# Combine and the last layer's attention in one pipeline, the context's LayerNorm beside the expert tiles

## The reference

```python
# layer 0, tail: combine the two experts' outputs of each token
eo = einsum('etf,efd->etd', gelu(einsum('td,edf->etf', x2, w1) + b1), w2) + b2
x3 = layernorm(x2 + sum_over_top2(weight[t, e] * eo[e, t]), ln3_g, ln3_b)
# layer 1, head: both sides of the attention are normalised with the same gain and shift
q_in = layernorm(x3, ln1_g, ln1_b)
kv_in = layernorm(ctx, ln1_g, ln1_b)
x4 = x3 + attention(q_in, kv_in, kv_in)      # 16 heads of 8, softmax over 64 keys
out = x4 + mlp(layernorm(x4, ln2_g, ln2_b))
```

## Time and profile before

| | |
|---|---|
| median of 3 runs | 1650.91 us (1648.1 to 1655.75) |
| the profiled execution, its own time | 1651.23 us |
| its span, first to last instruction | 1649.5 us |
| busy share of the span | PE 79%, PEld 65%, DVE 63%, ACT 56%, POOL 54% |
| mean granted TensorE clock | 0.882 of full |
| HBM traffic | 95.45 MB read, 50.86 MB written, 89 GB/s |

### The profile page before, as it was taken

How to read it: one execution, slowest core, us unless ns; L and a number is a source line. 1 busy time by engine, 2 the same in 40 slices (tenths; PEclk the granted TensorE clock), 3 DMA queues, 4 the chain that set the end, 5 groups by cost and what they waited for, 6 DMA issues and landing times. The chain is left out here.

```text
span 1649.5 us, 60559 instructions
## 1 busy us (share of the span) xinstructions
PE 1295.0 (79%) x23128; PEld 1068.0 (65%) x23128; DVE 1045.7 (63%) x2321; ACT 918.7 (56%) x1624; POOL 896.5 (54%) x1424
## 2 busy tenths in 40 slices
PE   5999999999999465799999980111138999994998
PEld 3787877778877364699999970111116788873676
DVE  4777777778878229677777762656636788782011
ACT  2787877788887305533333331544446788872333
POOL 2576767576676300477777737567504666753111
PEclk9999999999999757899999995555558999997899
DMA  3233333333332160022222213555522233321333
GB/s 104 83 91 102 89 101 93 104 91 103 107 95 72 46 211 0 22 65 61 61 60 60 60 45 97 136 144 144 150 96 65 86 107 102 96 78 43 106 114 90
DMA packets 169853, 147.65 MB, mean 90 GB/s; under 512 B 19105, under 2 KB 132257, under 8 KB 169761
## 3 DMA queue, kind: packets, MB, share of 16 engines
q1 hardware_dynamic: 161312, 129.11, 26.0%
q0 software_dynamic: 8448, 17.32, 4.5%
HBM read 95.45 MB, written 50.86 MB: 89 GB/s over the span
## 5 line engine op out<-in xcount | busy, mean ns | idle before, releaser
L741 DVE TENSOR_REDUCE at_mx<-at_ps_s 128x16 f32<-128x1024 f32 x128 | 156.1, 1220 | 104.5 <-PE at_ps_s L490 60.1
L1339 POOL DMA_INDIRECT ex_xg<-x,ex_ti x136 | 164.8, 1211 | 46.3 <-issue 44.6
L678 ACT ACTIVATE at_pt<-at_ps_t 128x1024 f32<-128x1024 f32 x128 | 130.6, 1020 | 52.5 <-PE at_ps_t L504 51.7
L1368 PE MATMUL ex_ps_y<-ex_wt,ex_hg 128*128 128x128 f32 x1088 | 157.2, 288 | 2.8 <-ACT ex_hg L1399 2.8
L671 ACT ACTIVATE at_pr<-at_dd 128x1024 f32<-128x1024 f32 x128 | 135.2, 1056 | 35.3 <-DVE at_dd L749 35.3
L749 DVE TENSOR_TENSOR at_dd<-at_ps_s,at_mx 128x1024 f32<-128x1024 f32 x128 | 153.7, 1202 | 0.1
L1551 POOL DMA_INDIRECT cb_yg<-rows,cb_sl x128 | 125.8, 983 | 44.4 <-issue 44.0
L1368 PEld LDWEIGHTS ex_ps_y<-ex_wt,ex_hg 128*128 128x128 f32 x1088 | 131.6, 191 | 26.0 <-ACT ex_hg L1399 21.8
L1359 PE MATMUL ex_ps_h<-ex_xt,ex_wt 128*128 128x128 f32 x1088 | 146.2, 278 | 0.0
L1391 ACT ACTIVATE ex_xt<-ex_ps_x 128x128 f32<-128x128 f32 x136 | 37.7, 277 | 193.8 <-issue 99.1
L504 PE MATMUL at_ps_t<-ident,at_pr 128*128 128x128 f32 x1024 | 138.9, 279 | 4.8 <-issue 3.3
(11 more groups left out here) (237 smaller groups left out, 3419.0 us busy)
## 6 DMA issues: line engine op xcount, KB each, us to landing
rows<-ex_y SPq DMA_DIRECT2D x136, 64.0 KB
x<-at_ln_out SPq DMA_DIRECT2D x32, 256.0 KB, 3.2
at_kx<-in_xt SPq DMA_DIRECT2D x16, 256.0 KB, 2.8
at_qx<-in_xt SPq DMA_DIRECT2D x16, 256.0 KB, 2.8
at_vin<-in_xt SPq DMA_DIRECT2D x16, 256.0 KB, 2.8
at_xr<-in_x SPq DMA_DIRECT2D x16, 256.0 KB, 3.0
x1t<-at_xt SPq DMA_DIRECT2D x16, 256.0 KB, 3.3
at_kx<-in_ctxt SPq DMA_DIRECT2D x16, 256.0 KB, 2.8
```

The source lines that it names most:

```text
L678: act.activation(pt[:, 2 * h + p], ps_t[:, :, :, :], ACT.Copy).then_inc(pt_ready, 1)
L741: dve.tensor_reduce(mx[:, p], ps_s[:, :, 4 * p:4 * p + 4, :], AX.X, ALU.max).then_inc(mx_ready, 1)
L1339: pool.indirect_dma_start(out=xg[:, s, :], out_offset=None, in_=x_src, in_offset=bass.IndirectOffsetOnAxis(ap=ti[:, s:s + 1], axis=0)).the ...
L1368: mm = pe.matmul(ps_y[s % 2][:, :], hg[:, s % 2, f, :], wt[:, s % HB, W2 + D * f:W2 + D * f + D], start=(f == 0), stop=(f == FC - 1))
```

## The change

combine_phase is gone. Its context part moves into expert_phase, once in each of the first 16 rounds of 8 tiles; the rest moves into a new fused_phase together with the last attention.

In the expert phase, round q normalises group q of the context: SP loads it at the round's first tile, VectorE takes statistics and moments at tiles 1 and 2, GpSimd computes the reciprocal root behind the gather of tile 7, ScalarE scales in two halves at tiles 4 and 5, TensorE transposes at tile 6, ScalarE copies at tile 7, SP stores. The PSUM bank for it comes from ps_h, which has 2 buffers in place of 4.

In the fused phase there are steps from -4 to 18. In step g the front of the pipeline weighs group g+4, finishes x3 of g+3 and z4 of g+2, whose transpose stays on the chip (qx) in place of going through HBM; the attention works on g, g-1 and g-2, and the last transpose is that of g-3. GpSimd fetches group g+5 in four portions between its other work, computes own and next LayerNorm's root together (front_rstd, eight columns), and no longer masks: ScalarE applies the head masks as scale and bias while it copies K and Q out of PSUM, in two passes each (kb, qb doubled). The context's group is loaded once for K and V. x3 goes to HBM and comes back for the residual. vx, ot, LayerNorm's out are doubled. The Sqrt and the Newton step are gone.

The diff, cut, in this order: the steps' loop; then, of fused_phase, the step of TensorE, two helpers and the step of ScalarE, a helper and the step of VectorE, two helpers and the step of GpSimd; then, of expert_phase, GpSimd, TensorE, ScalarE and VectorE; then the phases' calls. `prior`, `here`, `following` and `more` say whether group g-1, g, g+1 and g+2 exist, `front` whether g+4 does.

```diff
+def over_steps(eng, step, end):
...
+    for g in range(-4, 4):
+        step(At(1, g))
+    with eng.Fori(2, end // 2) as m:
+        for u in range(2):
+            step(At(1, m * 2 + u, 0, m * 2 + u, u, m))
+    for g in range(end, NG + 3):
+        step(At(1, g))
...
+                    if prior:
+                        turn(g * 2 - 1, 1, 1)
+                    if following:
+                        project_q(a.shift(1))
+                    if here:
+                        scores(a, 1)
+                        turn(g * 2, 0, 0)
+                    if prior:
+                        widen(g * 2 - 2, 0)
+                    if more:
+                        if following:
+                            pe.wait_ge(qb_ready, g + 2)
+                        else:
+                            pe.wait_ge(bob_ready, 1)
+                        project_k(a.shift(2))
+                    if prior:
+                        values(a.shift(-1), 1)
+                    if here:
+                        turn(g * 2, 0, 1)
+                    if following:
+                        if more:
+                            pe.wait_ge(kb_ready, g + 3)
+                        else:
+                            pe.wait_ge(qb_ready, g + 2)
+                        project_v(a.shift(1))
+                        scores(a.shift(1), 0)
+                    if a.shift(-3).exists():
+                        if following:
+                            pe.wait_ge(vx_ready, g + 2)
+                        elif a.shift(-2).exists():
+                            pe.wait_ge(y_ready, g - 1)
+                        else:
+                            pe.wait_ge(xt_ready, NG - 1)
+                        turn_x(a.shift(-3))
+                    if prior:
+                        widen(g * 2 - 1, 1)
+                    if here:
+                        turn(g * 2 + 1, 1, 0)
+                    if prior:
+                        if beyond(g, 2):
+                            pe.wait_ge(xt_ready, g - 2)
+                        else:
+                            pe.wait_ge(vx_ready, g + 2)
+                        project_out(a.shift(-1))
+                    if here:
+                        values(a, 0)
+                    if more:
+                        if prior:
+                            pe.wait_ge(y_ready, g)
+                        elif following:
+                            pe.wait_ge(vx_ready, g + 2)
+                        else:
+                            pe.wait_ge(kb_ready, g + 3)
+                        turn_z(a.shift(2))
...
+                def mask_q(a):
...
+                    for f in range(2):
+                        ins = act.activation(qb[:, a.u, :, f, :], ps_g[:, :].rearrange("p (b q) -> p b q", b=GB),
+                                             ACT.Identity, bias=side[:, 0, f:f + 1], scale=c.side[:, f:f + 1])
+                    ins.then_inc(qb_ready, 1)
...
+                def scale_next(a):
+
+                    act.wait_ge(fnb_ready, a.g + 2)
+                    if beyond(a.g, 1):
+                        act.wait_ge(z4t_ready, a.g - 1)
+                    front_scale(z4[:, a.u], x3[:, a.u], a.shift(1), NEXT).then_inc(fz_ready, 1)
...
+                    if following:
+                        copy_z(a.shift(1))
+                    if prior:
+                        exponent(g * 2 - 1, 1)
+                        copy_t(g * 2 - 1, 1, 0)
+                    if here:
+                        exponent(g * 2, 0)
+                    if prior:
+                        copy_t(g * 2 - 1, 1, 1)
+                    if following:
+                        mask_q(a.shift(1))
+                    if prior:
+                        copy_o(g * 2 - 2, 0)
+                    if here:
+                        exponent(g * 2, 1)
+                        copy_t(g * 2, 0, 0)
+                    if a.shift(3).exists():
+                        scale_own(a.shift(3))
+                    if a.shift(2).exists():
+                        mask_k(a.shift(2))
+                    if here:
+                        exponent(g * 2 + 1, 0)
+                        copy_t(g * 2, 0, 1)
+                    if following:
+                        copy_v(a.shift(1))
+                    if a.shift(-3).exists():
+                        copy_x(a.shift(-3))
+                    if prior:
+                        copy_o(g * 2 - 1, 1)
+                    if a.shift(2).exists():
+                        scale_next(a.shift(2))
+                    if a.shift(-2).exists():
+                        ln.act_scale(act, a.shift(-2))
+                over_steps(act, step, NG - 4)
...
+                def weigh_first(a):
+
+                    dve.wait_ge(yg_in[a.u], 16 * 2 * GP * (a.k + 1))
+                    dve.wait_ge(in_f[a.u], 32 * (a.k + 1))
+                    for t in range(GP):
+                        ins = dve.scalar_tensor_tensor(y1[:, a.u, t, :], yg[:, a.u, 0, t, :], wt[:, a.u, 0, t:t + 1],
+                                                       fx[:, a.u, t, :], ALU.mult, ALU.add)
+                    ins.then_inc(y1_ready, 1)
+
...
+                    if here:
+                        subtract(g * 2, 1)
+                    if a.shift(-2).exists():
+                        ln.dve_statistics(dve, a.shift(-2), y_ready)
+                    if prior:
+                        recip(g * 2 - 2, 0)
+                    if a.shift(-2).exists():
+                        ln.dve_moments(dve, a.shift(-2))
+                    if here:
+                        maximum(g * 2 + 1, 0)
+                    if prior:
+                        normalise(a.shift(-1), 0)
+                    if here:
+                        subtract(g * 2 + 1, 0)
+                    if front:
+                        weigh_first(a.shift(4))
+                    if here:
+                        maximum(g * 2 + 1, 1)
+                    if prior:
+                        recip(g * 2 - 1, 1)
+                    if here:
+                        subtract(g * 2 + 1, 1)
+                    if front:
+                        weigh_second(a.shift(4))
+                    if a.shift(3).exists():
+                        gain_own(a.shift(3))
+                    if following:
+                        maximum(g * 2 + 2, 0)
+                    if prior:
+                        normalise(a.shift(-1), 1)
+                    if a.shift(3).exists():
+                        shift_own(a.shift(3))
+                    if following:
+                        maximum(g * 2 + 2, 1)
+                        subtract(g * 2 + 2, 0)
+                    if front or a.shift(3).exists():
+                        front_statistics(a.shift(4))
+                    if prior:
+                        residual(a.shift(-1))
+                    if front or a.shift(3).exists():
+                        front_moments(a.shift(4))
...
+                def fetch_close(a):
+
+                    pool.wait_ge(fy_ready, a.g + 1)
+                    tick(2 + a.u)
...
+                def front_rstd(a):
+                    pool.wait_ge(fmv_ready, a.g + 1)
+                    if beyond(a.g, 1):
+                        pool.wait_ge(z3_ready, a.g - 1)
+                    if beyond(a.g, 2):
+                        pool.wait_ge(fz_ready, a.g - 2)
+                    pool.tensor_tensor(fneg[:, a.u, :], fmv[:, a.u, :, 0], c.minus_one[:, 0:2 * GP], ALU.mult)
+                    pool.tensor_tensor(frstd[:, a.u, :], fmv[:, a.u, :, 1], c.eps[:, 0:2 * GP],
+                                       ALU.add).then_inc(fvar_ready, 1)
+                    pool.wait_ge(fvar_ready, a.g + 1)
+                    pool.tensor_tensor(frstd[:, a.u, :], frstd[:, a.u, :], c.minus_half[:, 0:2 * GP],
+                                       ALU.pow).then_inc(frstd_ready, 1)
+                    pool.wait_ge(frstd_ready, a.g + 1)
+                    pool.tensor_tensor(fnb[:, a.u, :], fneg[:, a.u, :], frstd[:, a.u, :], ALU.mult).then_inc(
+                        fnb_ready, 1)
...
+                    nearby = a.shift(5)
+                    if a.shift(3).exists() or a.shift(2).exists():
+                        front_rstd(a.shift(3))
+                    if nearby.exists():
+                        fetch_open(nearby)
+                        fetch(nearby, 0, 1)
+                    if prior:
+                        spread(g * 2 - 2, 0)
+                    if nearby.exists():
+                        fetch(nearby, 1, 3)
+                    if a.shift(-2).exists():
+                        ln.pool_rstd(pool, a.shift(-2))
+                    if nearby.exists():
+                        fetch(nearby, 3, 5)
+                    if prior:
+                        spread(g * 2 - 1, 1)
+                    if nearby.exists():
+                        fetch(nearby, 5, 8)
+                    if a.shift(-2).exists():
+                        gain(a.shift(-2))
+                    if here:
+                        add_bias(a)
...
```

(33 more changed lines are left out.)

798 lines of the change are left out of this document (516 added, 282 removed).

## The result

| | median us | runs | ratio to before |
|---|---|---|---|
| before | 1651.97 (1648.1 to 1655.75) | 4 | |
| after | 1703.39 (1697.37 to 1705.57) | 4 | 1.0306 [1.0268, 1.0344] |
| predicted | 1567 (1528 to 1612) | | |

The change makes the kernel 3.1% slower; 5% faster was forecast. The profiled execution of after took 1705.57 us for a span of 1703.8.

What follows compares the result with a forecast made beforehand. GpSimd was taken to bound the fused stage. Experts ending at 1022.1 us, the fused stage at 1423.5 and the remaining 141.8 gave a span of 1565.3; with 1.7 outside it, 1567 us, range 1528 to 1612.

Steps and rivals of the forecast that it cites:

- The costly piece is an order on GpSimd's queue: Experts: the root waits for VectorE's moments, delaying the next gather; stall 1.4 us in a round of 2.3, 37 us total.
- part 1: The context's normalisation beside the expert tiles: 2.3 us a round, 16 rounds, 37 us.
- The upper bound of 55 us: Experts: the most part 1 could cost, if a whole weight copy held up both gather and root.
- The ring: Fused stage: chain from normalise through act_scale, gain and spread to the next normalise, 21.1 us; 22.5 taken per full group.
- the way to be wrong above all: Fused stage: a chain not followed, such as that of the one bank ps_g, is longer than 21 us.
- C: Rival, fused stage: GpSimd does not bind, VectorE's 18.6 us sets steps of 18.8; 1534 us, chance 0.12.
- The lists: Fused stage, work per group: GpSimd 20.4 us as the bound, VectorE 18.6, ScalarE 18.2, TensorE's matmuls about 14.
- A: Rival, experts: the gathers' lead is enough, the wait vanishes, a round costs 0.7 us; 1542 us, chance 0.17.
- B: Rival, fused stage: VectorE's instructions hold up GpSimd, full groups cost 4 us more; 1609 us, chance 0.14.
- D: Rival, fused stage: TensorE is granted 1.2 GHz, its 14 us become 25 to 28; 1687 us, chance 0.05.
- E: Rival, fused stage: each stage's chain waits wherever the other's runs, full steps take 28.7 us; 1639 us, chance 0.03.
- The light steps: Start of the fused stage: steps -3 to -1 add front_rstd to eight gathers and take 13.3 us each.

Runs made afterwards that it cites:

- e1: The kernel after with GpSimd's root of the context's variance moved behind the fifth tile's gather of the next round; 1655.49 us, ratio 1.0013.
- e2: e1 with the context's load also issued two tiles ahead of its round; 1643.28 us, ratio 0.9923 to before.
- f2: The kernel after with ScalarE's copy of the turned z moved behind two exponents and a copy of turned probabilities; 1671.31 us, ratio 1.0111.
- g2: g1 plus f3, against the kernel before; 1571.55 us, ratio 0.9508.
- g1: e2 and f2 together, against the kernel before; 1595.31 us, ratio 0.9653.
- f1: The kernel after with the fused stage's gathers left out and plain loads of the same sizes issued by SyncE instead; 1641.13 us, one run.
- f5: The kernel after with each fused-stage gather replaced by a GpSimd addition of constant rows that nothing reads; 1684.7 us, one run.
- f3: The kernel after with a fused step's last three gathers waiting until TensorE has turned back the output of three groups; 1692.81 us, ratio 1.022.

## Why the prediction was wrong

The span came out 138.5 us above the forecast of 1565.3. Against its sum:

| term of the sum | predicted | measured | off |
|---|---|---|---|
| expert tiles, last output | 1022.1 | 1067.6 | +45.5 |
| from there to the first front_rstd | 25.5 | 26.1 | +0.6 |
| steps -3 and -2 | 26.6 | 27.0 | +0.4 |
| steps -1, 0, 1 | 13.3, 15.5, 18.5 | 21.0, 22.2, 24.8 | +20.7 |
| steps 2 to 10 | 9 x 22.5 | 257.0 | +54.5 |
| steps 11 to 15 and on to the last residual | 99.5 | 114.4 | +14.9 |
| the rest | 141.8 | 143.7 | +1.9 |

**Step "The costly piece is an order on GpSimd's queue", 37 us.** The mechanism was right, sixteen times, and the gap, 2.05 us in the round shown and 2.1 in the mean, was 0.7 above the 1.4 taken. The gather left 6.4 us behind the transpose of step 8q+2 (741.71 to 748.15) where 5.3 was worked out, because VectorE's statistics had waited for their load. The term failed by what hangs on it: 1.2 us of half clock in the round shown and the like behind 12 other gaps, and 1 us for a context load issued at the round's start, which part 1 never timed ("nothing on it gets late" was said of ScalarE; of SyncE's load nothing was said). e1 measures gap and half clock at 52.4 us, e2 the load at 17.1. The upper bound of 55 us was too low for the same reason: the stage lost 79.6.

**Step "The ring", 22.5 us.** This is the step that turned the sign. The chain followed, from act_scale through gain to the spread, was not the longest. The longest one goes from the residual, which frees ps_g, through turn_z and copy_z into ScalarE's whole step; it was named as the way to be wrong above all, and not followed. f2 shows it: 3.2 us a step for one line of ScalarE's order. "If VectorE waits for scores while GpSimd idles, it is C": it did, with the opposite sign of C's, because the chain and not VectorE's list took over.

**The lists.** "TensorE gains four transposes; its matmuls without the waits between them are about 14 us" had gathers and bursts of small products on different engines at no price. Each gather beside such a burst costs it up to 1.4 us. That was in no list and in no rival, and could not be read from before: its gathers run in the combine with 17% of TensorE's time and beside the experts' large products. It is worth 2.6 us a step in g2 over g1, and explains part of steps -1 to 1: in step 0 eight gathers go out in a row and 32 scores last from 1151.44 to 1157.04, 5.6 us in place of the 1.17 of the earlier trace rows. Not all of it: without gathers, in f1, these three steps still take 56.8 us in place of the 47.3 forecast, and for that no cause is shown.

**Rivals.** A, B and C do not apply: the gather's lead was too short, GpSimd's 128x512 instructions kept 1.26 to 1.30 us and 64 of 72 gathers took under 1.12, and GpSimd did not bind. B also took VectorE as the engine that holds the other up, and in f5 it was VectorE that waited. D had the direction, and its sign (a granted clock under 0.9) is there at 0.85. But its full half clock is not; the slow stretches stand behind waits, and reorderings alone took the clock to 0.89 (f2, f3) and 0.98 (g2). So the low clock followed from the waits; how much of the 28.6 us it added no run separates. E's arithmetic, 12.8 + 15.84 = 28.7 us, is nearly what a full step measured, and that is a coincidence: the waits have the two causes above, and 5.8 us of them went with two reorderings.

**What held.** The light steps (13.3 us forecast, 13.5 measured), the power over eight columns between constant and proportional (1.67 us; the one over four 1.04), which gather is late, and the tail. With the orders of g2 a full step takes 22.8 us, which is the forecast's 22.5; that its whole time of 1571.6 us is near 1567 is luck in part, since it rests on experts that are 28 us shorter than the forecast's and on steps -1 to 1 that are longer.

## What to carry to other kernels

When two pipelines are put into one step, follow every shared bank from the instruction that frees it to the next that needs it, and look at what stands first in each engine's order: an instruction that waits for the step's last result must not stand ahead of work that is ready. A helper's arithmetic goes behind as much of the queue's lead as its reader allows, and a load that feeds a short chain goes a step ahead of it. Where a profile shows idle time ended by "issue" inside a burst of small matmuls, or by nothing the trace can name, look at what GpSimd issues at that moment and move it beside large products.
